# Row maxima of heads 1 to 3 as products over 128 contraction rows in place of 64

## What is computed

```python
g = jnp.einsum('bcn,bnm->bcm', fea, Wg)               # B=16, C=256, N=1024
q = relu(g * para)  ->  (B, heads=4, N, hd=64)
k, v = split(x @ kv_w)                                 # the same shape
attn = softmax(einsum('bhnd,bhmd->bhnm', q, k) * scale)
out = einsum('bhnm,bhmd->bhnd', attn, v)
x = layernorm(x + out)
```

## Time and profile before

| | |
|---|---|
| time, median of 3 runs | 3317.03 us (3315.31 to 3318.21) |
| profiled execution, its own time | 3317.71 us |
| its span | 3315.9 us |
| mean granted TensorE clock | 0.962 of 2.4 GHz |
| PE busy | 3002.8 us, 91% of the span |
| DVE busy | 2222.7 us, 67% |
| ACT busy | 1668.5 us, 50% |
| POOL busy | 1077.7 us, 33% |

### The profile page before, as it was taken

How to read it: one execution, slowest core, us unless ns; L and a number is a source line. 1 busy time by engine, 2 the same in 40 slices (tenths; PEclk the granted TensorE clock), 3 DMA queues, 4 the chain that set the end, 5 groups by cost and what they waited for, 6 DMA issues and landing times. The chain is left out here.

```text
span 3315.9 us, 38866 instructions
## 1 busy us (share of the span) xinstructions
PE 3002.8 (91%) x12436; PEld 1845.7 (56%) x12436; DVE 2222.7 (67%) x3015; ACT 1668.5 (50%) x1940; POOL 1077.7 (33%) x500
## 2 busy tenths in 40 slices
PE   6999999999999999999999999999959999997963
PEld 4454545545454544545454554545348888885853
DVE  6677777777687777777687777777543333336877
ACT  5455564546455564546455554646332222225768
POOL 1535243452535244353535344353620000000012
PEclk9999999999999999999999999999979999998986
DMA  4030211213031211213031211213023232325548
GB/s 134 12 115 26 89 57 57 63 51 95 19 114 36 78 57 57 64 50 110 11 107 38 76 57 57 74 40 89 1 95 115 76 114 76 114 75 200 196 154 281
DMA packets 168270, 276.13 MB, mean 83 GB/s; under 512 B 9761, under 2 KB 109089, under 8 KB 168225
## 3 DMA queue, kind: packets, MB, share of 16 engines
q1 hardware_dynamic: 168224, 275.55, 26.2%
HBM read 174.60 MB, written 67.11 MB: 73 GB/s over the span
## 5 line engine op out<-in xcount | busy, mean ns | idle before, releaser
L259 POOL TENSOR_TENSOR psum<-psum,probs 128x1024 f32<-128x1024 f32 x320 | 831.9, 2600 | 245.6 <-ACT probs L324 236.1
L324 ACT ACTIVATE probs<-sc_ps 128x1024 f32<-128x1024 f32 x512 | 524.5, 1024 | 732.2 <-PE sc_ps L786 730.5
L501 DVE TENSOR_REDUCE mx<-mx_ps 128x1 f32<-128x512 f32 x768 | 492.9, 684 | 199.2 <-PE mx_ps L754 197.0
L802 PE MATMUL pv_ps<-probs,v 128*64 128x512 f32 x2048 | 549.9, 615 | 2.8 <-ACT probs L324 2.6
L786 PE MATMUL sc_ps<-qa,ka 128*128 128x512 f32 x1024 | 451.1, 449 | 0.5 <-DVE qb L487 0.5
L786 PE MATMUL sc_ps<-qb,kb 128*128 128x512 f32 x1024 | 405.0, 401 | 0.0
L259 POOL TENSOR_TENSOR psum<-probs 128x1024 f32<-128x1024 f32 x64 | 152.2, 2378 | 757.8 <-ACT probs L324 393.6
L786 PEld LDWEIGHTS sc_ps<-qa,ka 128*128 128x128 f32 x1024 | 194.9, 192 | 291.1 <-issue 173.0
L754 PE MATMUL mx_ps<-ka,qa 64*128 64x512 f32 x768 | 296.3, 452 | 8.2 <-ACT v L312 2.7
L463 DVE SCALAR_TENSOR_TENSOR scr<-scr,adj_ring 128x1024 f32<-128x1024 f32 x128 | 219.8, 1718 | 102.4 <-ACT scr L292 99.9
L718 PE MATMUL sc_ps<-w_hi,x_hi 128*128 128x512 f32 x512 | 222.5, 434 | 59.0 <-DVE w_lo L468 58.6
(11 more groups left out here) (182 smaller groups left out, 5386.4 us busy)
## 6 DMA issues: line engine op xcount, KB each, us to landing
adj_ring<-in_adj_dram SPq DMA_DIRECT2D x128, 512.0 KB, 3.8
pre_scratch<-pre SPq DMA_DIRECT2D x32, 1024.0 KB, 4.2
hid<-pre_scratch SPq DMA_DIRECT2D x32, 1024.0 KB, 5.1
x<-in_x_dram SPq DMA_DIRECT2D x16, 1024.0 KB, 5.6
kb<-ka SPq DMA_DIRECT2D x64, 256.0 KB, 3.0
qa<-qa SPq DMA_DIRECT2D x64, 256.0 KB, 3.3
res<-in_x_dram SPq DMA_DIRECT2D x16, 1024.0 KB, 5.5
x_scratch<-res SPq DMA_DIRECT2D x16, 1024.0 KB, 4.3
```

Of the source, the lines that this page charges most:

```text
L259: pool.tensor_tensor(psum[:, :], probs[:, 0, :] if k == 1 else psum[:, :], probs[:, k % PR, :], ALU.add).then_inc(s["pool_added"], 1)
L324: nc.scalar.activation(probs[:, i % PR, :], sc_ps[:, t % 2, :], ACT.Exp, scale=SCALE)\
L501: nc.vector.tensor_reduce(mx2[:, nh, n:n + 1], mx_ps[:, nh, :], AX.X, ALU.max)\
L802: ins = nc.tensor.matmul(pv_ps[nh * HD:(nh + 1) * HD, h % 2, :], v[:, i, h * HD:(h + 1) * HD], probs[:, i % PR, nh * BANK:(nh + 1) * BANK] ...
```

## The change

For heads 1 to 3 the two products of a pair take all 128 rows of `qa[h]` and `ka[h]` in place of the 64 rows `own(h)`. The maximum is then that of leading query times whole key. Since the other 64 rows are now read, pair 0 waits for the DMA copy of the queries and for the trailing keys, in place of the leading queries alone. Head 0's maxima stay as they are. The order of the instructions on every engine stays the same.

```diff
                 elif n == 0:
                     wait(pe, s["row_done"], 4 * b + h)
-                    wait(pe, s["qh_done"], 4 * b + h + 1)
+                    wait(pe, qa_in[h], 16 * (b + 1))
+                    wait(pe, s["kl_done"], 4 * b + h + 1)
                     if h == 1:
                         wait(pe, s["v_evac"], 2 * b + 2)
...
                     out = mx_ps[:, nh, :] if h else sc_ps[:, n % 2, nh * BANK:(nh + 1) * BANK]
-                    nc.tensor.matmul(out, qa[h][own(h), n * P:(n + 1) * P], ka[h][own(h), nh * BANK:(nh + 1) * BANK],
+                    rows = slice(0, P) if h else own(h)
+                    nc.tensor.matmul(out, qa[h][rows, n * P:(n + 1) * P], ka[h][rows, nh * BANK:(nh + 1) * BANK],
                                      start=True, stop=True).then_inc(s["mx_ready"], 1)
```

## The result

The changed kernel takes 3287.43 us (median of 4 runs, 3286.98 to 3288.13) against 3317.11 us: a ratio of 0.9911, 95% interval 0.9894 to 0.9928. The profiled execution has a span of 3285.2 us and a mean granted clock of 0.968.

What follows compares the result with a forecast made beforehand. PE's own stream was taken to set the pace, except at merges, some DVE waits and between batches. Savings of 0.52, 0.62 and 0.54 us for heads 1 to 3 gave 26.9 us over 16 batches: 3290 us, range 3270 to 3304.

Steps and rivals of the forecast that it cites:

- the couples: Two pairs apart by scores only (0 and 1, 2 and 3, 5 and 6): typically save 0.16 us, not 0.40.
- the transposes: Behind pair 5 of heads 2 and 3: 0.10 us saved, perhaps 0.05 more at the transposes' own entry.
- head 3's first couple: Pairs 0 and 1 of head 3, where DVE is behind: bounds 0 and 0.16 us, taken as 0.08.
- the change of shape: PE switching between 128-row and 64-row products: 0.10 us a change; a pair saves 0.20 us if unhindered.
- the rival that waits make a pair dear: Rival "no change": the 0.20 us comes with every pair, for example from its waits; 3317 us, chance 0.06.
- Pair 4 of heads 2 and 3: Pair 3's reductions wait for the inversion, which waits for PE's transposes, so pair 4 saves 0.
- Pair 7: Last pair before the merge, which waits for POOL's add: saves 0; transpose stall grows 0.20 us to about 1.08.
- the gap ahead of POOL's add: Merge started 0.56 us after the add; reductions would end 0.20 us sooner, with 0.36 us missing.
- The rival "more": DVE's and POOL's gates give way: merge ahead of the add 3239 us, or all pairs but 7 saving 3250; chance 0.08.
- Head 1, 8.3 us: Head 1's maxima, made in head 0's steps: 0.52 us saved per batch, 8.3 us over 16 batches.
- the rival *slower: TensorE's clock falls at each of 48 merge stalls, 1.7 us lost each, 82 us: 3372 us; chance 0.04.

Runs made afterwards that it cites:

- The two runs with waits: 64-row kernel before plus pair 0's two new waits: 3317.41 us; changed kernel plus two long-met waits ahead of every product of pairs 1 to 7: 3288.54 us.
- halved reductions: DVE reduces 256 of 512 columns per half for heads 1 to 3: kernel before 3288.7 us, changed kernel 3183.17 us; with one-reduction merge too, 3246.69 and 3183.59 us.

## Why the prediction was right

The time was forecast at 3290 us and is 3287.4. The mechanism is right in its parts, and that the sum came within 3 us is in part luck, since three errors of size cancel. In the heads, where 26.9 us were forecast and 28.0 measured, the couples gave some 1.8 us less, the transposes 1.6 more and head 3's first couple 1.3 more. Step by step:

- *A 128-row product costs 0.23 us, and a pair loses 0.10 us at each side to the change of shape.* Right in sum: 0.23 us from score to pair, 0.55 us for the pair, 0.21 us less together. But the pair's change to the values stays and is part of its 0.55 us. The second half of the saving is inside the pair: its second product started 0.34 us after the first (979.24, 979.57) and now 0.23. The two runs with waits rule out the rival that waits make a pair dear.
- *A couple saves 0.16 us, since DVE's release takes the rest back.* Nearly right: 2.31 us where 2.28 was worked out, so that a couple saves 0.12 to 0.15 us; and 2.04 us with DVE out of the way, which is the unhindered number.
- *Pair 4 of heads 2 and 3 saves nothing.* Right, and for the reason given: the same pair still took 1.02 us with the merge as one reduction (999.58 to 1000.60), and fell to 0.55 us when only the inversion was moved behind pair 3's reductions.
- *Pair 7 saves nothing, and PE's stall grows to 1.08 us.* Right: 1.05 us, and the transpose kept its distance to step 5's first score. That POOL's add is what holds the merge is shown twice: by the same two-input merge, which takes 0.17 us where it comes ahead of the add, and by the merge with one input.
- *The merge misses the gap ahead of POOL's add by 0.36 us.* It misses it by 975.17 - 974.80 = 0.37 us. The rival "more" was thus a real one: with halved reductions it came true, 42 us in one step. I had its price nearly right (51 us with pair 7) but did not look for it when I set the expectation of the halved reductions.
- *Head 3's first couple saves 0.08 us.* Too small: it took 2.72 us before (1022.02 to 1024.74) and 2.56 after (1009.42 to 1011.98), 0.16 us. DVE's own chain ahead of it got shorter. Before, POOL's last add of head 1 stood 3.62 us (at 1015.97), since one of DVE's two operations of line 487 went ahead of it; now it takes 2.37 us (at 1003.21), both of DVE's come behind it, and DVE reaches `add_last` 0.16 us sooner after the transpose. This was only read from the traces. With the 0.05 us at the transposes that I left unclaimed, it makes up for head 3's 10.5 us against 8.6.
- *Head 1, 8.3 us.* 7.4 us measured. At the full clock the stretch went from 21.60 to 21.14 us, 0.46 us a batch where 0.52 was forecast; on what the clock adds, see below.
- *The clock.* No fall at the merges; the mean granted clock was 0.968 against 0.962. The price in the rival *slower*, 1.7 us a fall, was too high: a fall cost nothing between batches and 0.5 to 0.85 us in head 1's stretch, as the last section shows.

## What to carry to other kernels

Read the cost of a product from start to start, and look at what shape of the array stands on either side: here 64 rows in place of 128 saved nothing and cost 0.20 us for every run of them between full products, were it of two or of four. So a short contraction between full ones is better filled up with rows that are there anyway. Before counting such a gain over all instructions, ask at each place what the next wait hangs on: the 0.20 us was had in full at a pair alone; of a couple's 0.40 us only 0.12 to 0.16 were had, and nothing ahead of a merge tied to another engine. A tiny operation that always lasts as long as what is left of another engine's operation is held by it, and to make it a reduction of one input was worth more (45 to 49 us) than the change itself.

## What was not expected of the hardware

This is about the clock in head 1's stretch, behind a stall of 2.0 us that neither kernel changes. In the kernel before, half of the batches stayed at the full clock there and half fell to 1.2 GHz for a while, by turns: the stretch took 21.60 us in the one and 22.45 in the other. These windows of 10 us are of two batches in a row, with the granted clock behind the brackets of POOL.

```profile
965.00:975.00 10.00, 7.46 (x34) 4.00 (x33) 8.78 (x10) 8.00 (x12) 1.29 (x1) 1.00 0.62 185
1113.00:1123.00 10.00, 7.92 (x30) 5.14 (x31) 8.34 (x10) 8.18 (x12) 0.17 (x1) 0.83 0.64 188
```

In the changed kernel 14 of 16 batches fell, but earlier, so that more of the slow time lay in the stall: the products behind the stall are slow from the first on (0.21 us apart in place of 0.12), and the stretch took 21.6 us.

```profile
955.59 0.37 PE L765 MATMUL sc_ps<-ident,mxs 128*8 128x128 f32 x1 [2.03 <-DVE mxs L496]
955.62 0.56 PE L648 MATMUL mx_ps<-kvw_hi,xT_hi 128*128 128x256 f32 x1
955.98 0.42 PE L648 MATMUL mx_ps<-kvw_hi,xT_lo 128*128 128x256 f32 x1
956.19 0.41 PE L648 MATMUL mx_ps<-kvw_lo,xT_hi 128*128 128x256 f32 x1
```

With the full clock in both (the first batch) the stretch went from 21.61 to 21.14 us, 0.47 us where I had forecast 0.52. Falls cost 8 x 0.85 = 6.8 us before and, at some 0.49 us each, 6.8 us in the changed kernel's 14 batches. So the 7.4 us of head 1 are the mechanism, 16 x 0.46, and it is by chance that the clock took the same from both.

The falls between batches went away altogether. In the kernel before, the clock fell some 105 us after head 0's transpose in each of the first 15 batches (0.83 from 1070 to 1080 us); in the changed kernel it fell there in none. The window of the changed kernel at the same place:

```profile
1058.00:1068.00 10.00, 6.99 (x28) 4.50 (x29) 8.87 (x6) 5.74 (x7) 3.08 (x1) 1.00 0.53 190
```

This is where the mean clock of 0.968 against 0.962 comes from. It gave no time: the stretch that holds the place took 73.3 us a batch in both kernels. PE's products of `w_hi` wait there for DVE's `w_lo` (line 718, 58.6 us in all before and 80.0 after), so faster products only wait longer.

The change made each batch 1.8 us shorter, and with it moved when the fall comes; what decides it in a given batch was not tested and stays open.
